# Two separate seat lists, one per routing choice, for the first mixture of experts, with its results gathered in the stage itself, and a re-ordered graph layer behind it

## The reference

```python
x = x + _L0_gnn_ref(_layernorm(x), adj, ...)   # spectral graph layer (eigenvectors of adj)
x = x + _L0_ffn_ref(_layernorm(x), ...)        # mixture of 8 experts, two per token
x = x + _L1_gnn_ref(_layernorm(x), adj, ...)   # two graph convolutions, then LSTMs over windows of 1 to 4 nodes
x = x + _L1_ffn_ref(_layernorm(x), ...)        # mixture of 8 experts, one per token
# _L0_ffn_ref
top_w, top_i = jax.lax.top_k(xf @ Wg + bg, 2); top_w = softmax(top_w)
for e in range(8):
    h = gelu(xf @ W1[e] + b1[e])               # 128 -> 512
    out += w_dense[:, e:e+1] * (h @ W2[e] + b2[e])
```

## Time and profile before

| What | Value |
|---|---|
| median of 3 runs | 1651.18 us (1650.91 to 1659.6) |
| the profiled execution | 1653.19 us |
| its span in the profile | 1651.4 us |
| mean granted TensorE clock in it | 0.886 of full |
| busy share of PE, PEld, DVE, ACT, POOL | 74%, 53%, 52%, 46%, 36% |

### The profile page before, as it was taken

One profiled execution on the slowest core, in us unless ns is written; L12 is line 12 of the kernel. 1 busy time (PEld: TensorE's weight loads), 2 busy tenths in 40 slices (PEclk: granted clock), 3 DMA queues, 4 the chain that ended last, 5 costly groups with the idle time before them and its releaser, 6 DMA issues. The chain is left out here.

```text
span 1651.4 us, 26932 instructions
## 1 busy us (share of the span) xinstructions
PE 1229.3 (74%) x5977; PEld 874.8 (53%) x5978; DVE 860.5 (52%) x3547; ACT 763.9 (46%) x1920; POOL 599.2 (36%) x1015
## 2 busy tenths in 40 slices
PE   2444425487577999999487787999997897667776
PEld 1223314376566999998344343445443453656665
DVE  5777898856583222222466763444444675711111
ACT  3555534321175455545144444656554664633332
POOL 3666335200003556655577730000000000057775
PEclk9999855786589999999689889999999898589999
DMA  9300000001101222223122100000000332222221
GB/s 260 89 1 2 0 1 1 1 1 55 47 0 31 66 69 71 70 68 67 48 50 50 44 23 1 0 0 0 0 0 0 77 76 51 1 63 75 76 74 44
DMA packets 85697, 68.45 MB, mean 41 GB/s; under 512 B 18630, under 2 KB 74511, under 8 KB 85628
## 3 DMA queue, kind: packets, MB, share of 16 engines
q1 hardware_dynamic: 71228, 36.32, 9.0%
q0 software_dynamic: 14400, 31.39, 7.7%
HBM read 41.55 MB, written 26.64 MB: 41 GB/s over the span
## 5 line engine op out<-in xcount | busy, mean ns | idle before, releaser
L1493 POOL DMA_INDIRECT g_Z<-z,sitter x72 | 70.6, 980 | 507.8 <-SPq L1479 480.2
L1398 ACT ACTIVATE c_H<-ps,c_b 128x256 f32<-128x256 f32 x284 | 117.4, 471 | 133.5 <-PE ps L1427 132.6
L1342 POOL DMA_INDIRECT c_Z<-z,c_idx x142 | 138.2, 973 | 81.0 <-POOLq L1340 57.5
L1840 PE MATMUL ps<-BIG,w_ihT 128*128 x364 | 156.4, 579 | 5.2 <-ACTq L1853 5.2
L1628 POOL DMA_INDIRECT d_Y<-y,seat x128 | 130.2, 1017 | 60.7 <-issue 37.5
L1442 PE MATMUL ps<-w_dn,c_H 128*128 x1136 | 139.3, 276 | 3.4 <-ACT c_H L1398 3.0
L1427 PE MATMUL ps<-c_ZT,c_w 128*128 128x256 f32 x568 | 136.3, 383 | 1.4 <-ACT c_ZT L1386 1.4
L1442 PEld LDWEIGHTS ps<-w_dn,c_H 128*128 128x128 f32 x1136 | 132.4, 192 | 5.5 <-issue 5.2
L1840 PEld LDWEIGHTS ps<-BIG,w_ihT 128*128 128x128 f32 x364 | 69.8, 192 | 86.7 <-issue 86.7
L1376 DVE TENSOR_TENSOR c_ys<-ps,b_dn 128x256 f32<-128x256 f32 x71 | 30.2, 425 | 157.8 <-PE ps L1442 157.8
L1545 ACT ACTIVATE g_H<-ps,bias_cols 128x256 f32<-128x256 f32 x144 | 60.4, 471 | 111.2 <-PE ps L1582 110.4
(11 more groups left out here) (510 smaller groups left out, 2760.2 us busy)
## 6 DMA issues: line engine op xcount, KB each, us to landing
y<-c_ys SPq DMA_DIRECT2D x71, 128.0 KB, 1.8
z<-ZB SPq DMA_DIRECT2D x32, 256.0 KB, 2.6
z<-X SPq DMA_DIRECT2D x16, 256.0 KB, 4.2
c_Z<-z,c_idx POOLq DMA_INDIRECT x142, 2.6
w_up<-in_L_ffn_W_dram SPq DMA_DIRECT2D x1, 2048.0 KB
w_dn<-in_L_ffn_W_dram SPq DMA_DIRECT2D x8, 256.0 KB
w_dn<-in_L_ffn_Wd_dram SPq DMA_DIRECT2D x8, 256.0 KB
d_Y<-y,seat POOLq DMA_INDIRECT x128, 2.5
```

The lines of the kernel that those rows point to most:

```text
L1342: pool.indirect_dma_start(Z[u][:, h, :], None, z, bass.IndirectOffsetOnAxis(ap=idx[h][u][:, 0:1], axis=0)).then_inc(fetched[u], 16)
L1398: act.activation(H[u][:, c, :], UP[u][c // 2][:, c % 2 * SLOT_TILE:(c % 2 + 1) * SLOT_TILE], ACT.Gelu, bias=(b1[u] if w_up is not None els ...
L1493: pool.indirect_dma_start(Z[t % DEPTH][h][:, :], None, z, bass.IndirectOffsetOnAxis(ap=k.sitter[:, t * HALVES + h:t * HALVES + h + 1], axis=0)
L1840: last = pe.matmul(view(k.ps[4 * u + j], wide, lanes), k.w_ihT[:, w, :], state(i, u, s, p, wide, lanes), start=True, stop=(s == 0))
```

## The change

The first mixture's seats are sorted by choice first: 72 columns of 128 seats (`REGION`) for the first choices and 72 for the second. `route_choices` replaces `route` for it, and forms the inverse list transposed: `ohh` (72 columns) is now the weights and `above` (128 columns) moves, one half of `LIST` for each choice; two subtractions on VectorE and two transposes take the place of the `jump` matmul. The counts are bf16 matmuls. The table of experts is worked out behind the loop. `route` for the second mixture gets the same form. `above` comes from ScalarE's Sign and `ohh` from VectorE, as before.

`experts_in` replaces `experts`: 72 tiles of two 128-row halves, each half with its own expert. GpSimd's queue is written out. In the first 36 tiles it also fetches ahead the second halves of the last 36 into `k.BIG`; in the last 31 steps it fetches two tiles of first-choice results from `y0` instead, and VectorE adds them to `X`. `gnn1` gathers the second choice alone, with 14 buffers; VectorE weaves the combining and the statistics of a later group and `new_state` into the waits of `scale`, and ScalarE interleaves normalizations and gates, each with a semaphore step of its own.

```diff
-SLOTS0 = (2 * B * N + E * (SLOT_TILE - 1)) // SLOT_TILE * SLOT_TILE
+REGION = -(-((B * N + E * (P - 1)) // P) // 2) * 2
+SLOTS0 = 2 * REGION * P
-AHEAD = 8
+AHEAD = 14
+Y_RING = 8
@@ spectrum, layer_gnn0
-            pool.memset(k.jump[:, :], 0.0).then_inc(s_pool, 1)
-            for n, (away, value) in enumerate(((0, 0.5), (1, -0.5), (1 - P, 0.5))):
...
+            dve.tensor_copy(k.ones16[:, :], k.ones[:, :])
+            dve.tensor_copy(k.upper16[:, :], k.upper[:, :])
@@ route_choices, vector
+            for c in range(n):
+                dve.tensor_copy(M[:, c, :, :], by_expert(choices[c])).then_inc(marks, 1)
...
+            for c in range(n):
+                got = link.put(dve.tensor_tensor_scan(flat(S, c), ones[:, :], TOT[c][:, :], 0.0, ALU.mult, ALU.add))
...
+            for c in range(n):
+                got_slot = link.put(tt_(flat(slot, c), flat(S, c), RANK[c][:, :], ALU.add))
...
+            link(ts_(blocks[:, :], blocks[:, :], P.bit_length() - 1, None, ALU.logical_shift_right))
...
+            link(dve.tensor_copy(seats, pos[:, :]))
+            got_low = link.put(ts_(low[:, :], seats, P - 1, None, ALU.bitwise_and))
...
+                    ts_(ohh[b][:, :], k.irow[:, c * REGION:(c + 1) * REGION], hi[:, ds(t + c * TILES, 1)], half_token[:, ds(t, 1)],
+                        ALU.is_equal, ALU.mult).then_inc(oh_ready, 1)
...
+            link(dve.tensor_copy(summed[:, :, :], LIST.rearrange("s (c q) -> s c q", c=n)))
+            tt_(own_seats[:, :, 1:P], by_row[:, :, 1:P], by_row[:, :, 0:P - 1], ALU.subtract).then_inc(s_kept, 1)
+            tt_(own_seats[:, :, 0:1], by_row[:, :, 0:1], by_row[:, :, P - 1:P], ALU.add).then_inc(s_kept, 1)
+            link.need(got)
+            link(dve.tensor_reduce(out=ef[:, :], in_=te[:, :, :], axis=AX.X, op=ALU.add))
@@ route_choices, tensor
+                    pe.matmul(LIST[:, c * P:(c + 1) * P], ohh[b][:, :], above[b][:, :],
+                              start=False, stop=False).then_inc(oh_used, 1)
...
+                last = pe.transpose(SEATS[:, c * REGION:(c + 1) * REGION], own_seats[:, c, :], k.ident[0:REGION, 0:REGION])
@@ experts_in
+        def experts_of(eng, t):
+            both = eng.value_load(k.expert[0:1, ds(t, 1)], min_val=0, max_val=E * E - 1)
+            return [both // E, both % E]
...
+            for t in range(2, NT):
+                pool.wait_ge(turned, t - 1)
+                fetch(t, 0)
+                if t < SECOND:
+                    fetch(t, 1)
+                    fetch_ahead(SECOND + t)
...
+                if t > COMBINE:
+                    for m in range(2):
+                        fetch_result(2 * (t - COMBINE - 1) + m)
...
+            def step(s, j, q, staging, combining):
...
+                    weights(s + 1, 1 - u, None if early else s * PER, None if early else s * PER)
+                if staging and (not known or s + 2 < NT):
+                    stage(s + 2, u)
+                if combining:
+                    for n in range(2):
+                        combine(s * 2 + (n - 2 * COMBINE), 2 * j + n, q - COMBINE // 4 + 1)
+                if not known or s > 0:
+                    biased(s - 1, 1 - u, q * 2 + (j - 1) // 2 if j else q * 2 - 1)
...
+                    for h in range(HALVES):
+                        o = c % 2 * SLOT_TILE + h * P
+                        act.activation(H[u][:, c, h * P:(h + 1) * P], UP[u][c // 2][:, o:o + P], ACT.Gelu,
+                                       bias=b1[u][h][:, c:c + 1]).then_inc(gelu, 1)
...
+                    for c in range(C):
+                        for h in range(HALVES):
+                            o = c % 2 * SLOT_TILE + h * P
+                            pe.matmul(UP[u][c // 2][:, o:o + P], w1[u][h][:, c * P:(c + 1) * P], ZT[u][:, h * P:(h + 1) * P],
+                                      start=True, stop=True).then_inc(up, 1)
@@ gnn1, gpsimd and vector
-                for f in range(2):
-                    pool.indirect_dma_start(Y[b][f][:, :], None, y,
...
+                pool.indirect_dma_start(Y[b][:, :], None, y,
...
+            def scale(g, beside, state):
...
+                rows(0, combine)
...
+                    if turn == 1 and state >= 0:
+                        new_state(state)
...
+            for g in range(GROUPS + 2):
                 if 1 <= g <= GROUPS:
                     add_bias(g - 1)
+                if g >= 2:
                     new_cell(g - 2)
+                if g + 2 < GROUPS:
+                    scale(g + 2, g + 3, g - 2)
+                elif g >= 2:
+                    new_state(g - 2)
@@ gnn1, scalar
+                if g >= 2:
+                    new_tanh(g - 2)
+                ahead = 1 <= g < GROUPS - 1
+                if ahead and g > 1:
+                    normalized(g + 1, range(2))
...
+                    gate(g - 1, 0)
+                if ahead:
+                    normalized(g + 1, range(2 if g > 1 else 0, 3))
+                if 1 <= g <= GROUPS:
+                    gate(g - 1, 1)
+                    gate(g - 1, 2)
+                if ahead:
+                    normalized(g + 1, range(3, 4))
```

More of the change, by code:

```diff
@@ L1175, in _, with route @@
             sweep(pe, step, tail=2)
-def route(nc, k, sem, tag, choices, slots, block, beside=None):
+def route(nc, k, sem, tag, choice, slots, beside):
     marks, counted, oh_ready, ab_ready, oh_used, listed, placed = (
         sem(f"{tag}_{n}") for n in "marks counted oh ab used listed placed".split())
[L1183 to L1186, removed]
+    cols_ = slots // P
+    RANK, TOT, SEATS = k.ps[0], k.ps[1], k.ps[3]
+    LIST = k.ps[2][0:cols_, 0:P]
     s_kept, s_beside = sem(f"{tag}_kept"), sem(f"{tag}_beside")
@@ L1234, in _ @@
[L1234 to L1239, removed]
@@ L1301, in _ @@
-            pe.matmul(LIST[:, 0:cols_], k.ident[:, :], zero[:, :], start=True, stop=False)
+            for what, mat in ((TOT, k.ones16), (RANK, k.upper16)):
+                for c in range(n):
+                    pe.wait_ge(marks, c + 1)
+                    last = pe.matmul(what[c][:, :], mat[:, :], M[:, c, :, :].rearrange("p e t -> p (e t)"), start=True, stop=True)
+                last.then_inc(counted, 1)
+            pe.wait_ge(placed, 1)
+            pe.matmul(LIST, zero[:, :], ones[:, 0:n * P], start=True, stop=False)
@@ L1309, in _ @@
-            pe.matmul(SEATS[:, 0:cols_], k.jump[:, :], summed[:, :], start=True, stop=True).then_inc(listed, 1)
-def experts(nc, k, sem, tag, z, y, slots, w_up_all, w_up, w_dn, b_up, b_dn):
-    w_ready, turned, turned_sb, up, gelu, dn, y_ready, copied = (
-        sem(f"{tag}_{n}") for n in "w turned turned_sb up gelu dn y copied".split())
-    fetched, stored = ([sem(f"{tag}_{n}{u}") for u in range(2)] for n in ("fetched", "stored"))
+                    pe.matmul(LIST[:, c * P:(c + 1) * P], ohh[b][:, :], above[b][:, :],
+                              start=False, stop=False).then_inc(oh_used, 1)
@@ new lines, in _, with paired @@
+            pe.matmul(LIST, zero[:, :], ones[:, 0:n * P], start=False, stop=True).then_inc(listed, 1)
+            pe.wait_ge(s_kept, 2)
+            for c in range(n):
+                last = pe.transpose(SEATS[:, c * REGION:(c + 1) * REGION], own_seats[:, c, :], k.ident[0:REGION, 0:REGION])
+            last.then_inc(listed, 1)
+def paired(eng, step, first, stop):
+    with eng.Fori(0, (stop - first) // 2) as i:
+        for j in range(2):
+            step(i * 2 + (first + j), j, i + first // 2, first)
@@ L1447, in _ @@
+            for m in range(2 * (NT - COMBINE - 1), TILES):
+                fetch_result(m)
         @block.sync
@@ L1660, in scale @@
[L1660 to L1664 removed]
+                link.put(tt_(v, v, v, ALU.mult))
+                rows(1, combine)
+                link.need(got_both + 1)
@@ new lines, in scale @@
+                rows(2, combine)
+                for turn in range(3):
+                    link.need(got)
+                    got = link.put(tt_(t, out, half[:, :], ALU.mult))
+                    if turn == 0:
+                        rows(3, combine)
+                    link.need(got)
+                    got = link.put(tt_(t, t, out, ALU.mult))
+                    if turn == 0:
+                        rows(2, stats)
+                    if turn == 1 and state >= 0:
+                        new_state(state)
+                    link.need(got)
+                    got = link.put(stt(out=out, in0=t, scalar=1.5, in1=out, op0=ALU.add, op1=ALU.mult))
+                    if turn == 0:
+                        rows(3, stats)
```

621 lines of the change are left out of this document (383 added, 238 removed).

## The result

The changed kernel takes 1574.97 us in the median of 4 runs (1573.15 to 1575.46), beside 1651.79 us for the kernel before. The ratio of the means is 0.9523, with a 95% interval of 0.9498 to 0.9549. On the 1651.18 us of the runs shown ahead of the prediction that is 1572.4 us: faster, as forecast, but by 77 to 79 us where 53 were forecast, and just under the range's low end of 1574 (the median itself lies just above it). The likeliest case was given as 1598.

A forecast was written before the change was run, and what follows sets the result against it. TensorE was taken to bound `experts`, and a chain of waits `gnn1`. The terms -58 + 16 - 3.3 - 8 = -53.3 us took the median from 1651.2 to 1598 us, range 1574 to 1628.

The forecast's parts named there:

- group time: In `gnn1`: 8.0 us a group, from TensorE's 7.5 us plus 0.5 us for the last normalization.
- ramp and tail: In `gnn1`: 36 us before, taken as 40 us because three groups are prepared before the loop turns.
- GpSimd leads by a little: In `experts`: GpSimd's gathers, copy delays and a wait take 3.93 us a step, above TensorE's 3.79; stage +16 us.
- The 0.07 a pair: In `experts`: each pair of VectorE copies costs a GpSimd gather 0.07 us, so 0.14 us a step.
- I take -0.5: Loop of route t: -0.5 us, between at best -5 if the wider operand lifts the clock and +3 if not.
- Seats: Seat calculation of route r: 14.5 us in place of 20.60, a change of -6.1 us.
- the handshake: Loop of route r: ScalarE goes on pacing it, with +1 us for the handshake.
- Three: Whole kernel at its better bounds: 7.5 us a `gnn1` group, 3.79 us an experts step; about 1576 us, chance 0.08.
- One: In `gnn1`: a chain, not TensorE, paces groups at 9.5 to 10 us; about 1624 us, chance 0.17.
- Two: In experts: VectorE or ScalarE holds the step to 4.3 to 4.5 us; about 1630 us, chance 0.14.
- Four: In experts: copies block GpSimd for their whole length, 5.0 us a step; about 1675 us, chance 0.02.
- Five: In `gnn1`: TensorE falls to half clock, its 7.5 us becoming 14; about 1690 us, chance 0.02.

## Why the prediction fell short

**gnn1.** The mechanism and the group time (8.0; 7.95) were right, and the run with the old order shows both. What failed is the step that took 40 us for ramp and tail "as three groups are now prepared": 154.25 - 15 x 7.95 = 35.0 us. The first mix, 17.5 us into the stage before (794.53 to 812.02), now comes 11.9 us into it (792.83 to 804.74), since four gathers, not eight, precede it. I counted the groups prepared and not the gathers that the change had just halved. The run with two gathers a tile bears this out: there the first mix comes 16.9 us into the stage. This is 5 us. Timelines of before and after:

```profile
812.02 2.08 PE L1761 MATMUL ps<-BDAT,ZB 128*128 128x128 f32 x8 [20.98 <-ACT ZB L1712]
```
```profile
804.74 2.08 PE L2025 MATMUL ps<-BDAT,ZB 128*128 128x128 f32 x8 [15.62 <-ACT ZB L1961]
```

**Experts.** The step that failed is "GpSimd leads by a little", 3.93 us: the 0.14 us charged for copies and 0.05 for a wait on top of 3.73. In 65 steps this makes up 9 of the 24 us missed. The 0.07 a pair came from one gather of 1.02 us. The lines view, which groups all gathers, has the better row (first before, then after):

```profile
L1342 POOL DMA_INDIRECT c_Z<-z,c_idx x139 | 134.9, 970 | 78.9 <-POOLq L1340 55.7 <-issue 23.3
```
```profile
L1476 POOL DMA_INDIRECT c_Z<-z,sitter x108 | 102.8, 952 | 253.3 <-POOLq L1306 204.1 <-issue 25.0 <-PE ps L1633 24.1
L1489 POOL DMA_INDIRECT c_rows<-y,seats x64 | 62.4, 975 | 19.5 <-issue 19.5
```

The mean gather was 970 ns before, 0.03 above 0.94: three such with their issue take 3.81 us, a tie with TensorE's 3.79 and not a lead. In the changed kernel three take 3.77 us in the first half (mean 953 ns from 510 to 640 us) and 3.81 in the second. The run with the fourth gather measures the surcharge by itself: 0.06 us a step in the first half and 0.12 in the second, not 0.19. The term was right in kind and about two to three times too large, and GpSimd's head start, which the prediction did not count, hides what is left of it in the second half.

**Route t.** The step that failed is "I take -0.5" for the loop. The case itself was named ("if the wider moving operand lifts the clock ... at best -5"), and it came, at -6.0. Its bound was mis-sized too: 64 patterns at the prediction's own 0.33 to 0.40 us take 21 to 26 us, which is -3 to -7.5 on 28.6. The windows had shown the other loop, with 142 columns moving, at 0.94 beside this one at 0.50, and that comparison argued for the rise; I took a value between the two cases instead. The padded list in the kernel before shows that padding alone is enough in this loop. Why the clock is granted so is not settled here.

**Route r.** Seats -7.5 where -6.1 was taken: the first pattern comes after 13.0 us, not 14.5. The 0.9 us taken for the entry do not show, as the stage begins with the first copy, and the three pairs of 128x512 operations took 1.2 us each, not 1.4. The loop fell by 2.0 us where +1 was taken: the handshake does not show, ScalarE's patterns are 0.324 us apart (40.20 us for 124), and the clock comes up sooner, 0.63 and 1.00 in the loop's first two stretches of 4 us, 0.50 and 0.80 before. Why sooner was not tested. The tail grew by 2.6 where 1.8 was taken.

**The rivals.** Three (all bounds favourable, 1576) has the total that came, and had 0.08, but not for its reasons. Its 3.79 us a step in the experts came true; its 7.5 us a group in `gnn1` did not (7.95), and the shorter ramp made up for most of that; the two routes gained 3.9 and 3.3 us more than its -3 and -11. That its sum agrees is in good part luck. Its bounds had also been treated as if they had to come together, and each was more likely than that by itself. One (a chain paces `gnn1`) is out: TensorE waits 0.27 us a group. Two (VectorE or ScalarE holds up the experts' step) is out for this kernel, though its wait for VectorE's weights appears as soon as the copies are doubled. Four, copies that block GpSimd for their length, is excluded by the doubled copies. Five is out: the clock of `gnn1` rose from 0.83 to 0.91.

## What to carry to other kernels

Price an interference from the row that groups all its instances, not from the instance that shows it best. When two engines come within a few per cent of each other, the larger sum is not yet the bound: give the tie its own case. When stages are shortened, recount what runs ahead of the loop as well as the loop.

Where a loop keeps TensorE busy at half the granted clock, a padded operand or the other order of the two is worth a run: here more work took 6 us out of 28.6.

## What was not expected of the hardware

A VectorE operation with both inputs in SBUF holds up a gather much more than a copy does. `new_state` (1.02 to 1.05 us, 128x512) made the gather that starts beside it take 1.34 us in the changed kernel and 1.63 us with two gathers a tile, against 0.94. The kernel before had it too: beside the `new_state` at 909.44 the gather at 909.67 takes 1.50 us. In all three the gather is longer by about 0.23 us less than the part of `new_state` that was still to run (863.91 - 863.27 = 0.64 and 0.40 longer; 865.53 - 864.61 = 0.92 and 0.69 longer; 910.46 - 909.67 = 0.79 and 0.56 longer), as if it went on for 0.23 us, stood still until VectorE was done, and then finished. The other groups agree but for one, in the changed kernel at 830.44, whose gather took 0.95 us. Copies cost a gather far less: in the first half of `experts_in` gathers take 0.94 to 1.05 us, and up to 1.19 with the copies doubled. The Trainium skill, page SBUF — State Buffer, section "Who interferes with whom", says that a VectorE instruction with two SBUF inputs contends with a GpSimd instruction that reads SBUF; the 1.63 us agree. It says the same, as a full block, of copies in a 2-port mode; no such block shows in any run here, though none shows either in which mode the copies ran, and the measurement decides.
